# Bias and map of the fourth row group by GpSimd, in a binarised 3x3 convolution on one core

## The chip, the cores and the metric

The program runs on one core of a Trainium2 chip. The metric is the device time of one execution in microseconds (us). Three executions of the kernel before took 914.83, 915.45 and 915.15 us, a median of 915.15 us.

## The reference

The input `x` has 16 images of 256 channels and 56 x 56 pixels, in f32. It is normalised over groups of 8 channels, then by batch statistics over all images. The sign `t` (+1 or -1) of the result goes through a 3x3 convolution with 256 output channels, a bias is added, and every pixel is multiplied by a map that has one value per pixel for all channels. The input is added at the end:

```
t  = sign(xn)
xc = clip(xn, -1, 1)
y  = conv3x3(t, conv_w) + conv_b
beta_map = (box3x3(sum_c(xc * t)) + beta) / (box3x3(sum_c |t|) + beta)
out = x + y * beta_map
```

The change concerns the last two steps of `y`: "add the bias, multiply by the map".

## The kernel before, in words

**Start.** Up to 134 us the images are loaded once for their statistics, and the weights are scaled and transformed. GpSimd does 30 operations on the weights there, all done by about 101 us.

**Images and groups.** Each image has four groups g = 0..3: g % 2 is the half of the channels (256 = 2 x 128 partitions), g // 2 the upper or lower 28 rows. A group is a 128 x 1568 f32 tile `y[:, g]`. The convolution is done in a transformed form over the rows: TensorE makes six planes per group in three pairs, 24 matmuls each. In the steady loop PE takes, for each g of image n, `first(n, g)`, `third(n, g - 1)` and `second(n, g)`: 72 matmuls a slot, 288 an image. After `first(n, 0)` (in image 1 after `third(0, 3)`) it makes `quarter_sums` (L688), two small matmuls for the map of image n. `first(n, g)` waits until the accumulator pair that it writes into has been read: `y03_done` at 4n + g - 1, which is the end of `ends(n, g - 2)` on VectorE (L735, 736).

**VectorE (DVE)** works off a written list. Its pieces are:
- `transform(n + 1, g)` (L994 to 1016): the six input planes of a group of the next image, from the tile `T`; f16 operations, most with two inputs in SBUF.
- `mid(n, g)` (L1055 to 1069): two of every four output rows of a group, from ScalarE's snapshots `sn` of the accumulators. It waits for `y_out[g]`, the previous image's store out of `y[:, g]`.
- `ends(n, g)` (L1071 to 1079): the other two rows, read from the accumulators in PSUM and the tile `ds` in SBUF. It signals `y03_done`.
- `finish(n, g)` (L1081 to 1088): bias and map in one operation over 128 x 1568, in place in `y[:, g]`. It signals `scaled`.
- `pair_sum` (L1030) and `fold` (L1037): sums for the map; `beta_map(n)` (L1043 to 1052): the map of image n. It waits for `crow`, which comes by two DMAs from the quarter sums.

The order in the steady loop (`begin` and `proceed`) for an image n is: finish(n-1, 1), transform(n, 3), mid(n-1, 3), ends(n-1, 3), beta_map(n); finish(n-1, 2), transform(n+1, 0), mid(n, 0), ends(n, 0), pair_sum(n+1, 0); **finish(n-1, 3)**, fold(n+1, 0), transform(n+1, 1), mid(n, 1), ends(n, 1); finish(n, 0), pair_sum(n+1, 1), transform(n+1, 2), mid(n, 2), ends(n, 2), fold(n+1, 1). In image 1, `beta_map(1)` comes after ends(1, 0).

**ScalarE (ACT)** makes the signs, the tile `T`, the absolute values, and the snapshots.

**GpSimd (POOL)** only issues DMAs after the start. Its queue runs over s = 4n + g: wait until `y[:, g]` is scaled, issue the DMA that adds `x` to it (L385), then wait until the add before that has landed and issue its store to `out` (L380).

**SyncE (SP)** issues the loads of `x`, the DMAs of the sums, and the loads of the map into `bmap`: `map_load(n, 1)`, the lower half, waits until finish(n-1, 3) is done with the half that it overwrites (L289 to 295).

The last image's group 3 has code of its own (`last_mid`, `last_end`, `last_finish`).

Of the kernel before, what the change touches and what calls it, by code (L numbers as in the profile page):

```python
# [49 lines left out]
def conv_preact(nc, x, w_t, consts, sum_rows, map_rows, out):  # L50
# [6 lines left out]
    with ExitStack() as ctx:  # L57
# [3 lines left out]
        def sem(name):  # L61
            return ctx.enter_context(nc.semaphore(name))
# [96 lines left out]
            sem(s) for s in ("first_done", "second_done", "third_done", "snap1", "snap2"))  # L159
        ds_done, mid_done, y03_done, scaled, last_added = (  # L160
            sem(s) for s in ("ds_done", "mid_done", "y03_done", "scaled", "last_added"))

        WA = 13
        WP = 15
# [5 lines left out]
        def at_least(eng, s, value):  # L170

            if not (isinstance(value, int) and value <= 0):
                eng.wait_ge(s, value)
# [62 lines left out]
        @block.sync  # L236
        def _(sp):
            def stat_load(k):

                m, a, c = stat_image(k)  # L240
                if k >= BUFFERS:
                    block_read(sp, k - BUFFERS)
                sp.dma_start(stat_buffer(k), x_rows[m, c]).then_inc(s_in[k % BUFFERS], 16)

            def load_rows(src, g):

                h = g // 2
                first = (HR - 1) * W * h
                sp.dma_start(xb[:, g % 2, h], src[g % 2, :, first:first + XR * W]).then_inc(x_in[g], 16)

            stat_load(0)
            stat_load(1)
            for c in range(CT):
                sp.dma_start(wt[:, c], w_v[:, c].rearrange("p (a b o) -> p a b o", a=3, b=3)).then_inc(w_in[c], 16)
            for k in range(2, 2 * NI - 2):
                stat_load(k)
            for c in range(CT):
                block_read(sp, (2 * NI - 3) // BUFFERS * BUFFERS + c)
                for g in (c, 2 + c):
                    first, at = (HR - 1) * W * (g // 2), (UPPER - 1 + g // 2) * W  # L260
                    for lo, hi, s in ((0, at, x_upper[g]), (at, XR * W, x_in[g])):
                        sp.dma_start(xb[:, c, g // 2, lo:hi], x_rows[0, c][:, first + lo:first + hi]).then_inc(s, 16)

            def crow_load(m):

                sp.wait_ge(cs8_ready, m + 1)
                sp.dma_start(sum_rows[m, W:W + H * W].rearrange("(k f) -> k f", f=SQ), cs98[:, :])\
                  .then_inc(cs_stored, 16)
                sp.wait_ge(cs_stored, 16 * m + 16)
                at_least(sp, vsum_ready, m)  # L270
                sp.dma_start(crow[:, :, 1:W + 1], row_windows[m].rearrange("r (k w) -> r k w", w=W))\
                  .then_inc(crow_in, 16)

            def load(n, src, g):

                sp.wait_ge(u_ready, 4 * n + g + 4)
                sp.wait_ge(abs_done, 4 * n + g + 5)
                load_rows(src, g)

            def first_load(g):  # L280

                if g:
                    sp.wait_ge(u_ready, g)
                else:
                    sp.wait_ge(u0_ready, 1)
                sp.wait_ge(abs_done, g + 1)
                load_rows(x_rows[1], g)

            def map_load(n, h):  # L289

                if h:
                    at_least(sp, scaled, 4 * n)
                sp.dma_start(bmap[:, h, :],
                             map_rows[n:n + 1, h * HPX:(h + 1) * HPX].to_broadcast([P, HPX]))\
                  .then_inc(bmap_in[h], 16)

            def map_store(n):

                sp.wait_ge(bm_ready, n + 1)
                sp.dma_start(map_rows[n].rearrange("(r w) -> r w", w=W), bm[:, :]).then_inc(bm_stored, 16)  # L300
                sp.wait_ge(bm_stored, 16 * n + 16)

            def image(n, ahead=None):

                crow_load(n)
                if ahead is not None:
                    load(n, ahead, 0)
                map_store(n)
                map_load(n, 0)
                if ahead is not None:  # L310
                    load(n, ahead, 1)
                map_load(n, 1)
                if ahead is not None:
                    load(n, ahead, 2)
                if ahead is not None:
                    load(n, ahead, 3)

            for g in range(G4):
                first_load(g)
            sp.wait_ge(zeros_in, 16)  # L320
            image(0, x_rows[2])
            for n in range(1, NI - 2):
                image(n, x_rows[n + 2])
            image(NI - 2)
            image(NI - 1)

            sp.wait_ge(last_added, 1)
            sp.dma_start(out_v[NI - 1, 0, 1], y[:, 2]).then_inc(last_out[2], 16)
            for k, (lo, hi) in enumerate(LAST_ROWS):
                sp.wait_ge(last_added, k + 2)  # L330
                sp.dma_start(quads(out_v[NI - 1, 1, 1])[:, :, lo:hi].rearrange("p q i w -> p q (i w)"),
                             quads(y[:, 3])[:, :, lo:hi].rearrange("p q i w -> p q (i w)")).then_inc(last_out[k], 16)
            for g in range(G4):

                sp.wait_ge(y_out[g], 16 * (NI - (g > 1)))
            for k in range(3):
                sp.wait_ge(last_out[k], 16)


        @block.gpsimd  # L340
        def _(pool):
            done = [0]

            def after_own():

                pool.wait_ge(w_pool, done[0])

            def signal(ins):
                ins.then_inc(w_pool, 1)
                done[0] += 1  # L350


            pool.wait_ge(wscale, 1)
            for ci in range(CT):
                w0, w1, w2 = (wt[:, ci, d] for d in range(3))
                E, PP, QQ, G0, G2, HH = (wtmp[:, k] for k in range(6))
                for dy in range(3):
                    signal(nc.gpsimd.tensor_tensor(
                        wt[:, ci, dy], wt[:, ci, dy], scl[:, None, :].to_broadcast([P, 3, C]), ALU.mult))
                if ci:  # L360
                    pool.wait_ge(w_act, WA * ci)
                after_own()
                signal(nc.gpsimd.tensor_tensor(E, w0, w2, ALU.add))
                after_own()
                signal(nc.gpsimd.tensor_tensor(PP, E, w1, ALU.add))
                signal(nc.gpsimd.tensor_tensor(QQ, E, w1, ALU.subtract))
                pool.wait_ge(w_act, WA * ci + 3)
                signal(nc.gpsimd.tensor_tensor(G0, G0, G2, ALU.add))
                after_own()
                signal(nc.gpsimd.tensor_tensor(G2, G0, HH, ALU.add))  # L370
                signal(nc.gpsimd.tensor_tensor(HH, HH, G0, ALU.subtract))

                for o, (k, src) in enumerate(((0, w0), (5, w2), (1, PP), (2, QQ), (3, G2), (4, HH))):
                    pool.wait_ge(w_act, WA * ci + 7 + o + 1)
                    signal(nc.gpsimd.tensor_tensor(U[:, ci, 1, k], src, U[:, ci, 0, k], ALU.subtract))
            def store(s):

                n, g = divmod(s, G4)
                pool.wait_ge(x_added[g], 16 * n + 16)
                pool.dma_start(out_v[n, g % 2, g // 2], y[:, g]).then_inc(y_out[g], 16)  # L380

            for s in range(G4 * NI - 2):
                n, g = divmod(s, G4)
                pool.wait_ge(scaled, s + 1)
                pool.dma_start(y[:, g], x_v[n, g % 2, g // 2], accum_op=ALU.add).then_inc(x_added[g], 16)  # L385
                if s:
                    store(s - 1)
            store(G4 * NI - 3)


# [408 lines left out]
        def _(dve):  # L799
# [289 lines left out]

            def add_x(g):  # L1090

                dve.wait_ge(scaled, G4 * NI - 3 + g)
                nc.vector.tensor_tensor(y[:, g], y[:, g], own_rows(g), ALU.add).then_inc(last_added, 1)

            def last_mid():
# [32 lines left out]
            def last_finish(k):  # L1128
# [3 lines left out]
                dve.wait_ge(bmap_in[1], 16 * NI)  # L1132
                nc.vector.scalar_tensor_tensor(out=part(y[:, 3]), in0=part(y[:, 3]), scalar=vec[:, 2, 1:2],  # L1133
                                               in1=part(bmap[:, 1]), op0=ALU.add, op1=ALU.mult).then_inc(scaled, 1)
                dve.wait_ge(scaled, G4 * NI + k)
                nc.vector.tensor_tensor(part(y[:, 3]), part(y[:, 3]), part(own_rows(3)), ALU.add)\  # L1136
                  .then_inc(last_added, 1)

# [33 lines left out]
            def proceed(n, a, map_after=False):  # L1172
                before = lambda g, back: (n, g - back) if g >= back else (n - 1, 4 + g - back)
                for g in range(1, G4):
                    finish(*before(g, 3))
                    if g == 3:
                        pair_sum(n + 1, 1)
                    if g == 2:
# [28 lines left out]
            finish(last - 1, 2)  # L1207
            mid(last, 0)
            ends(last, 0)
            finish(last - 1, 3)  # L1210
            mid(last, 1)
            ends(last, 1)
            finish(last, 0)
# [46 lines left out]
```

## Time and profile before

| | |
|---|---|
| median of three executions | 915.15 us |
| the profiled execution's own time | 915.17 us |
| its span (first to last instruction) | 913.4 us |
| PE busy | 783.5 us, 86% |
| DVE busy | 767.3 us, 84% |
| ACT busy | 647.2 us, 71% |
| POOL busy | 139.7 us, 15% |
| mean granted clock | 0.939 |

The span is the time from the first to the last instruction of the profiled execution; 1.8 us of its own time lie around it. A busy share is an average over the start, the loop and the tail, which have different limits; POOL's counts the issuing of its DMAs.

### The profile page before, as it was taken

How to read it: one execution, taken by the hardware profiler on the slowest of the kernel's cores; microseconds unless marked ns; L12 is line 12 of the kernel's file. 1: busy time of each engine (PE TensorE's matmuls, PEld its weight loads, DVE VectorE, ACT ScalarE, POOL GpSimd, SP SyncE). 2: the span in 40 equal slices, each digit the busy share in tenths (PEclk: the TensorE clock that was granted, in tenths of full speed). 3: DMA queues.
4: the chain of work that ended last, by engine and by line, in shares of the span. 5: the costliest groups of instructions: out<-in, count | busy, mean ns of one | idle time of the engine just before them, and what ended most of it. 6: DMA issues, size and time to landing. Idle time of an engine off the chain costs nothing.

```text
span 913.4 us, 12806 instructions
## 1 busy us (share of the span) xinstructions
PE 783.5 (86%) x4722; PEld 468.0 (51%) x4722; DVE 767.3 (84%) x1193; ACT 647.2 (71%) x516; POOL 139.7 (15%) x158
## 2 busy tenths in 40 slices
PE   2100019999999999999999999999999999999996
PEld 2100015555555555555555555555555555555554
DVE  4899689999797888888888889797979797979756
ACT  2365638889696978777777777788878696969411
POOL 0089400011011111111111001111111110101011
PEclk9655559999999999999999999999999999999999
DMA  9999962399897888878888879796959696867578
GB/s 381 429 429 427 427 271 78 122 262 269 253 277 218 242 258 241 227 254 229 250 236 228 266 195 305 171 327 157 319 153 307 183 298 195 287 177 213 142 215 246
DMA packets 44874, 232.06 MB, mean 254 GB/s; under 512 B 10928, under 2 KB 11952, under 8 KB 40752
## 3 DMA queue, kind: packets, MB, share of 16 engines
q0 software_dynamic: 17856, 99.56, 41.9%
q1 hardware_dynamic: 26800, 132.05, 38.8%
q8 instruction: 14, 0.23, 0.1%
q10 hardware_dynamic: 192, 0.12, 0.0%
q14 instruction: 12, 0.10, 0.0%
HBM read 179.92 MB, written 51.79 MB: 254 GB/s over the span
## 4 chain that ended last, share of the span: by engine, by line
PE 72%; DVE 1%; DMA 1%; issue 1%; ACT 1%; DVEq 0%; ACTq 0%
PE acc L702 72%; DMA sum_rows<-cs 1%; DVE y L1133 0%; DMA crow<-sum_rows 0%; ACT r L519 0%; DVE y L1076 0%; ACT low L494 0%; PE low L688 0%; ACT r L525 0%; DVE y L1123 0%; DVE D L1008 0%; DVE ds L1060 0%; DVE y L1136 0%; ACT sn L637 0%; DVE ds L1104 0%
## 5 line engine op out<-in xcount | busy, mean ns | idle before, releaser
L702 PE MATMUL acc<-V,U 128*128 128x385 f16 (+1 forms) x4608 | 761.7, 328 | 0.9 <-DVE y L1076 0.4
L702 PEld LDWEIGHTS acc<-V,U 128*128 128x128 f16 x4608 | 449.9, 98 | 308.5 <-issue 1.5
L545 ACT ACTIVATE sn<-acc,inv_s 128x784 f32<-128x784 f32 x126 | 114.4, 908 | 162.7 <-PE acc L702 158.5
L385 POOL DMA_DIRECT2D y<-x x62 | 53.3, 859 | 702.5 <-DVE y L1087 689.1
L504 ACT ACTIVATE T<-low 128x2352 f16<-128x2352 f32 x60 | 127.3, 2122 | 0.9 <-DVE D L1008 0.9
L1087 DVE SCALAR_TENSOR_TENSOR y<-y,cst,bmap 128x1568 f32<-128x1568 f32 x63 | 115.5, 1833 | 0.1
L519 ACT ACTIVATE r<-xb,ab 128x1568 f32<-128x1568 f32 x64 | 106.6, 1690 | 5.5 <-ACT low L494 4.0
L494 ACT ACTIVATE low<-xb,ab 128x1624 f32<-128x1624 f32 x60 | 102.2, 1703 | 0.2
L508 ACT ACTIVATE T<-T 128x1568 f16<-128x1568 f16 x58 | 87.6, 1510 | 1.9
L662 PE MATMUL low<-mv,cst 128*128 128x32 f32 x2 | 0.6, 396 | 85.0 <-DVE mv L822 85.0
L1008 DVE TENSOR_TENSOR D<-T 128x1568 f16<-128x1568 f16 x60 | 58.3, 972 | 13.9 <-ACT T L508 13.8
L1060 DVE SCALAR_TENSOR_TENSOR ds<-sn 128x784 f32<-128x784 f32 x63 | 60.9, 967 | 4.0 <-ACT sn L545 4.0
L1037 DVE TRANSPOSE_TENSOR_REDUCE quarter<-ssum 128x49 f32<-128x1568 f32 x32 | 57.7, 1803 | 0.1
L1030 DVE SCALAR_TENSOR_TENSOR ssum<-r 128x1568 f32<-128x1568 f32 x32 | 57.1, 1785 | 0.3
L380 POOL DMA_DIRECT2D out<-y x62 | 50.0, 807 | 12.3 <-DMA y<-x 10.8
L525 ACT ACTIVATE r<-r 128x1568 f32<-128x1568 f32 x32 | 48.4, 1511 | 1.0
L1000 DVE TENSOR_SCALAR T<-T 128x784 f16<-128x784 f16 x60 | 21.3, 355 | 30.0 <-ACT T L504 30.0
L1065 DVE SCALAR_TENSOR_TENSOR y<-sn,ds 128x392 f32<-128x392 f32 x63 | 35.8, 568 | 10.9 <-DMA out<-y 4.5
L662 PEld LDWEIGHTS low<-mv,cst 128*128 128x128 f32 x2 | 0.5, 309 | 85.1 <-issue 85.1
L1076 DVE SCALAR_TENSOR_TENSOR y<-acc,inv_s,ds 128x392 f32<-128x392 f32 x63 | 39.0, 618 | 3.9 <-PE acc L702 3.9
L1043 DVE TENSOR_REDUCE vsum<-crow 56x58 f32<-56x174 f32 x16 | 5.5, 346 | 40.3 <-DMA crow<-sum_rows 40.3
L834 DVE BATCH_NORM_STATS2 st<-xb 128x6 f32<-128x448 f32 x63 | 34.1, 605 | 6.2 <-DMA xb<-x 6.1
(153 smaller groups left out, 517.8 us busy)
## 6 DMA issues: line engine op xcount, KB each, us to landing
xb<-x SPq DMA_DIRECT2D x60, 812.0 KB, 6.6
y<-x POOLq DMA_DIRECT2D x62, 784.0 KB, 8.5
out<-y POOLq DMA_DIRECT2D x62, 784.0 KB, 9.6
bmap<-map_rows SPq DMA_DIRECT2D x32, 784.0 KB, 6.5
xb<-x SPq DMA_DIRECT2D x10, 1568.0 KB, 18.7
y<-x SPq DMA_DIRECT2D x10, 1568.0 KB, 18.0
r<-x SPq DMA_DIRECT2D x5, 1568.0 KB, 18.0
sn<-x SPq DMA_DIRECT2D x5, 1568.0 KB, 19.0
```

The source lines that it names most:

```text
L385: pool.dma_start(y[:, g], x_v[n, g % 2, g // 2], accum_op=ALU.add).then_inc(x_added[g], 16)
L494: nc.scalar.activation(signs[:, 1:1 + XR], by_row(xb[:, c, g // 2]), ACT.Sign, scale=ab[:, a, 0, c:c + 1], bias=ab[:, a, 1, c:c + 1])\
L504: nc.scalar.activation(taps[:, 2:8].rearrange("p k (w q) -> p k w q", q=Q), row_taps(g), ACT.Relu, scale=2.0).then_inc(t_ready, 1)
L508: nc.scalar.activation(taps8, taps[:, 2:6], ACT.Copy, scale=4.0, bias=-3.0).then_inc(t8_ready, 1)
L519: nc.scalar.activation(r[:, c, 0:HPX], own_rows(g), ACT.Abs, scale=ab[:, a, 0, c:c + 1], bias=ab[:, a, 1, c:c + 1]).then_inc(abs_done, 1)
L545: nc.scalar.activation(kept, sums, ACT.Copy, scale=inv_s[:, b:b + 1]).then_inc((snap1, snap2)[half], 1)
L702: return nc.tensor.matmul(into, U[:, ci, digits, k, dx, co * P:(co + 1) * P], plane, start=(planes is FIRST and i == 0), stop=(planes is T ...
L1008: nc.vector.tensor_tensor(diff[:, 0], taps[:, 4:8], taps8, ALU.subtract).then_inc(cq_done, 1)
L1030: nc.vector.scalar_tensor_tensor(out=ssum[:, :], in0=r[:, 0, 0:HPX], scalar=1.0, in1=r[:, 1, 0:HPX], op0=ALU.min, op1=ALU.subtract).then_i ...
L1037: nc.vector.tensor_reduce(quarter[:, h, :], ssum[:, :].rearrange("p (b i) -> p b i", i=SQ), AX.X, ALU.add, apply_transpose=True).then_inc( ...
L1060: nc.vector.scalar_tensor_tensor(out=ds[:, :, :], in0=sn[:, b, 0], scalar=2.0, in1=sn[:, b, 1], op0=ALU.mult, op1=ALU.subtract).then_inc(d ...
L1087: nc.vector.scalar_tensor_tensor(out=y[:, g], in0=y[:, g], scalar=vec[:, 2, b:b + 1], in1=bmap[:, h], op0=ALU.add, op1=ALU.mult).then_inc( ...
```

## The change

The bias and map of group 3 of images 0 to 14 become two operations of GpSimd (`finish_3`): a tensor_scalar that adds the bias in place, a wait for its own signal, and a tensor_tensor that multiplies by the map in place. VectorE's finish(n, 3) goes. GpSimd starts with them when it comes to s = 4n + 3 in its queue and group 3's rows are complete; it no longer waits for VectorE there. `scaled` counts three groups an image, and the new `scaled_3` the fourth; the waits of SyncE and of the tail are adapted. Group 3 of the last image stays with VectorE.

```diff
             def map_load(n, h):
                 if h:
-                    at_least(sp, scaled, 4 * n)
+                    at_least(sp, scaled, 3 * n)
+                    at_least(sp, scaled_3, n)
...
+            def finish_3(n):
+
+                pool.wait_ge(mid_done, 4 * n + 4)
+                pool.wait_ge(y03_done, 4 * n + 4)
+                nc.gpsimd.tensor_scalar(y[:, 3], y[:, 3], vec[:, 2, 1:2], None, ALU.add).then_inc(raised, 1)
+                pool.wait_ge(raised, n + 1)
+                pool.wait_ge(bmap_in[1], 16 * n + 16)
+                nc.gpsimd.tensor_tensor(y[:, 3], y[:, 3], bmap[:, 1], ALU.mult).then_inc(scaled_3, 1)
+                pool.wait_ge(scaled_3, n + 1)
...
             for s in range(G4 * NI - 2):
                 n, g = divmod(s, G4)
-                pool.wait_ge(scaled, s + 1)
+                if g == 3:
+                    finish_3(n)
+                else:
+                    pool.wait_ge(scaled, 3 * n + g + 1)
                 pool.dma_start(y[:, g], x_v[n, g % 2, g // 2], accum_op=ALU.add).then_inc(x_added[g], 16)
...
             def add_x(g):
-                dve.wait_ge(scaled, G4 * NI - 3 + g)
+                dve.wait_ge(scaled, (G4 - 1) * NI - 2 + g)
...
-                dve.wait_ge(scaled, G4 * NI + k)
+                dve.wait_ge(scaled, (G4 - 1) * NI + 1 + k)
...
                 for g in range(1, G4):
-                    finish(*before(g, 3))
+                    if g != 2:
+                        finish(*before(g, 3))
...
             ends(last, 0)
-            finish(last - 1, 3)
             mid(last, 1)
```

## Rows read from the trace of the kernel before

**Rows 1.** The page's first part: busy time, share of the span, instructions.
```profile
span 913.4 us, 12806 instructions
PE 783.5 (86%) x4722; PEld 468.0 (51%) x4722; DVE 767.3 (84%) x1193; ACT 647.2 (71%) x516; POOL 139.7 (15%) x158
```
**Rows 2.** Windows of one image's length: busy us (instructions) of each engine, granted clock.
```profile
431.00:478.50 47.50, 47.50 (x292) 28.33 (x291) 40.56 (x57) 37.42 (x29) 5.67 (x8) 1.00 0.83 240
```
**Rows 3.** The chain that ended last, in order of time: start us, us, what.
```profile
307.14 1.17 DVE y L1076 x2
308.31 0.14 issue
308.45 27.81 PE acc L702 x168
...
573.96 47.40 PE acc L702 x288
```
**Rows 4.** Matmul timeline, image 9: start us, us, what.
```profile
573.68 0.28 PE L688 MATMUL low<-cst,quarter 128*98 128x32 f32 x2
573.79 47.56 PE L702 MATMUL acc<-V,U 128*128 128x392 f16 x288
621.20 0.28 PE L688 MATMUL low<-cst,quarter 128*98 128x32 f32 x2
```
**Rows 5.** VectorE's timeline, image 9.
```profile
582.84 0.35 DVE L1043 TENSOR_REDUCE vsum<-crow 56x58 f32<-56x174 f32 x1 [2.59 <-DMA crow<-sum_rows]
583.90 1.84 DVE L1087 SCALAR_TENSOR_TENSOR y<-y,cst,bmap 128x1568 f32<-128x1568 f32 x1
...
587.59 0.57 DVE L1013 TENSOR_TENSOR V<-D 128x784 f16<-128x784 f16 x1
...
591.07 0.62 DVE L1076 SCALAR_TENSOR_TENSOR y<-acc,inv_s,ds 128x392 f32<-128x392 f32 x1
591.60 0.62 DVE L1076 SCALAR_TENSOR_TENSOR y<-acc,inv,ds 128x392 f32<-128x392 f32 x1
592.13 1.79 DVE L1030 SCALAR_TENSOR_TENSOR ssum<-r 128x1568 f32<-128x1568 f32 x1
593.84 1.85 DVE L1087 SCALAR_TENSOR_TENSOR y<-y,cst,bmap 128x1568 f32<-128x1568 f32 x1
...
597.33 0.32 DVE L1000 TENSOR_SCALAR T<-T 128x784 f16<-128x784 f16 x1
...
603.34 0.61 DVE L1076 SCALAR_TENSOR_TENSOR y<-acc,inv,ds 128x392 f32<-128x392 f32 x1
```
**Rows 6.** Matmul timeline, quarter sums of images 1, 3 and 4.
```profile
196.52 0.36 PE L688 MATMUL low<-cst,quarter 128*98 128x32 f32 x2
...
288.27 0.28 PE L688 MATMUL low<-cst,quarter 128*98 128x32 f32 x2
...
336.10 0.28 PE L688 MATMUL low<-cst,quarter 128*98 128x32 f32 x2
```
**Rows 7.** VectorE's timeline, images 1 and 3.
```profile
211.59 0.61 DVE L1076 SCALAR_TENSOR_TENSOR y<-acc,inv,ds 128x392 f32<-128x392 f32 x1
...
298.92 0.35 DVE L1043 TENSOR_REDUCE vsum<-crow 56x58 f32<-56x174 f32 x1 [3.84 <-DMA crow<-sum_rows]
```
**Rows 8.** Waits of PE, 140 to 240 us: us in total, times, longest.
```profile
PE acc L702 <- DVE y L1076: 0.4, 1, 0.4
```
**Rows 9.** GpSimd's groups by form: busy us, mean ns | idle before.
```profile
L385 POOL DMA_DIRECT2D y<-x x62 | 53.3, 859 | 702.5 <-DVE y L1087 689.1 <-issue 13.4
L371 POOL TENSOR_TENSOR V<-V 128x768 f32<-128x768 f32 x2 | 3.6, 1806 | 0.0
```
**Rows 10.** VectorE's groups by form.
```profile
L1087 DVE SCALAR_TENSOR_TENSOR y<-y,cst,bmap 128x1568 f32<-128x1568 f32 x63 | 115.5, 1833 | 0.1
L1022 DVE TENSOR_SCALAR u<-xb,AB,neg_b 128x1624 f16<-128x1624 f32 x1 | 1.1, 1124 | 0.0
```
**Rows 11.** GpSimd's timeline, image 9.
```profile
586.03 0.86 POOL L385 DMA_DIRECT2D y<-x  x1 [12.60 <-DVE y L1087]
586.59 0.87 POOL L380 DMA_DIRECT2D out<-y  x1
595.98 0.85 POOL L385 DMA_DIRECT2D y<-x  x1 [8.53 <-DVE y L1087]
596.90 0.56 POOL L380 DMA_DIRECT2D out<-y  x1
```
**Rows 12.** VectorE's groups, 44 to 62 us, beside GpSimd's operations.
```profile
L834 DVE BATCH_NORM_STATS2 st<-sn 128x6 f32<-128x448 f32 x7 | 3.8, 601 | 0.0
```
**Rows 13.** VectorE's groups, 104 to 120 us, GpSimd idle.
```profile
L834 DVE BATCH_NORM_STATS2 st<-y 128x6 f32<-128x448 f32 x14 | 7.5, 604 | 3.2 <-DMA y<-x 3.2
```
**Rows 14.** Windows in the tail and in the warm-up; the third number from the end is the granted clock.
```profile
909.00:913.40 4.40, 0.00 (x0) 0.00 (x0) 1.19 (x2) 0.00 (x0) 0.00 (x0) 0.81 0.63 182
```

More of the change, by code:

```diff
@@ L161, in conv_preact @@
             sem(s) for s in ("ds_done", "mid_done", "y03_done", "scaled", "last_added"))
+        raised, scaled_3 = sem("raised"), sem("scaled_3")
         WA = 13
```

## The prediction

> **What bounds the kernel now.** I read the engines' busy times first: PE 86%, DVE 84% [rows 1]. These average over the start, so next came windows of one image's length in the loop: PE is busy for all of 47.50 us at full clock, DVE for 40.56, ACT for 37.42, POOL for 5.67 [rows 2]. The chain of waits says the same: unbroken pieces of 288 matmuls, 47.40 us each [rows 3]. TensorE sets the time from 225 us on. A faster VectorE gives it nothing; a later one costs, once it is later than its margin.
>
> So the question is how large that margin is. In image 9 the quarter sums start at 573.68 us and the next ones 47.52 us later; the 288 matmuls between take 47.41 us, 0.1646 us each [rows 4]. `first(9, 2)` stands 120 matmuls after the quarter sums, at 573.79 + 19.75 = 593.54 us. It needs `ends(9, 0)`, whose second operation ends at 591.60 + 0.61 = 592.21 us [rows 5]. Image 3 shows what happens without margin: the last operation of ends(3, 0) ends at 308.31, PE starts 0.14 us later at 308.45 [rows 3], and that image takes 336.10 - 288.27 = 47.83 us [rows 6] where image 9 takes 47.52. So the result must be there 0.14 us early, and the margin in image 9 is 593.54 - 0.14 - 592.21 = **1.2 us**. The stretch before it is tied to PE: the map's `crow` lands at 582.84 us, 9.16 us behind the quarter sums, and from there VectorE has no gap up to 592.21, 9.4 us [rows 5]. A delay in that stretch is not worked off before PE needs the result, and as `crow` follows PE's quarter sums, the stretch begins as late as PE does in the next image: each image pays anew. In image 3 `crow` came 10.65 us behind [rows 6, 7], hence no margin. In image 1, where the sums stand 24 matmuls later, ends(1, 0) ends at 212.20 [rows 7] and is needed at 196.52 + 0.11 + 96 x 0.1646 - 0.14 = 212.29 [rows 6]: 0.1 us.
>
> **The change, part by part.**
>
> *Taken from VectorE:* 15 operations of 1833 ns [rows 10], 27 us. In image 9 it is the one at 593.84 us [rows 5], behind ends(9, 0), so it widens the margin of the next slot alone. PE waits there once, for 0.4 us in image 1 [rows 8]: worth 0.4 us; elsewhere the matmuls hide it.
>
> *Added to GpSimd, the product:* a tensor_tensor over 768 f32 takes 1806 ns [rows 9], so 1568 take 1.806 x 1568 / 768 = 3.7 us.
>
> *Added to GpSimd, the bias:* no row shows a tensor_scalar there. From above, 3.7 us, the rate of the tensor_tensor; from below 1.1 us, VectorE's one-input f32 operation over 1624 [rows 10]. The nearest row is GpSimd's own, and the new operation has one input stream where that has two: I take half of it, 1.85 us. The Trainium skill (GPSIMD Engine Reference, 4.1 Engine selection) says that GpSimd's one-input elementwise work runs at roughly line rate, and its section 3 gives 1.03 cycles an element at 1.2 GHz, by which I estimate 1.35 us; the forecast would then be about 7 us lower.
>
> *Where they run:* GpSimd's queue comes to group 3 of image 8 after the add of group 2 (586.03 us) and the store behind it, which ends at 587.46 [rows 11]. Group 3's rows are then long complete. So the two operations begin at 587.5 us, amid VectorE's gapless stretch (L1013 starts at 587.59), and need 1.85 + 3.7 = 5.55 us: to 593.1, past the end of ends(9, 0).
>
> *What stands queued behind:* the add of x (595.98 us before) and the store of group 2 (596.90) [rows 11]. Alone, GpSimd would be done by 593.3, so both go out no later than before; cost nothing. SyncE's map load for the lower half waits for the same point, also no later. Should GpSimd take 5 us more, both go out some 2 us late, with the whole slot of 11.9 us until `mid` of the next group needs the store.
>
> *What they do to VectorE:* this is the disputed term. Between 587.5 and 591.07 us nearly all its operations (V<-D, ds, the two of `mid`) read two tiles in SBUF. The trace has no such operation beside GpSimd's arithmetic. It has only one-input ones: bn_stats takes 601 ns beside GpSimd's tensor_tensors and 604 ns with GpSimd idle [rows 12, 13], no loss. For two inputs the loss L lies between nothing and the whole 5.55 us (VectorE standing still while GpSimd works); a gain is excluded, as the removed operation lies behind ends(n, 0). Only the first 1.2 us are free, so four fifths of the interval cost time. I take the upper end, L = 5.55 us: GpSimd and VectorE each work in place over whole rows, and what one has in one-input operations is no measure of it. The Trainium skill (SBUF — State Buffer, Who interferes with whom) says that a VectorE instruction with two SBUF inputs contends with a GpSimd instruction that reads SBUF, since its second input comes through a read interface that they share, and that whichever starts second waits for the whole of the first. The one-input rows agree with that page's other half, that a one-input instruction outside the two-port modes is not held up; no row here shows the two-input case.
>
> *The sum:* images 2 and 4 to 14 (12 images): 12 x (5.55 - 1.2) = 52.2 us. Image 1: 5.55 - 0.1 = 5.45. Image 3: 5.55. Image 15 has no transforms, and its ends wait for PE: 0. The wait in image 1: -0.4. Together 62.8 us. Against the profiled execution, 915.17 us (span 913.4 and 1.8 around it; 0.02 over the median), that is **978 us**. With the bias at 1.1 us it is 14 x 0.75 = 10.5 less, 967.5; with 3.7 us 25.9 more, 1004.
>
> **The rivals.** 0.2% of the time, 1.8 us, is about what a measurement of this kernel can tell from no change.
>
> *A. Hidden, not slower.* GpSimd and VectorE do not hold each other up, or VectorE keeps precedence while its operations follow without a gap. Then GpSimd's bias falls in the free place, the two operations of `ends` at 591.07 [rows 5], which read one tile from PSUM. It ends at 592.9, holds pair_sum (592.13) by 0.8 us; the product begins behind pair_sum at 594.7 and ends at 598.4, beside the fold; the next transform begins 1.1 us later than its 597.33, and ends(9, 1), 603.95 before, ends at 605.0 where PE needs it at 593.54 + 11.85 - 0.14 = 605.25. PE never waits. The time is 915.2 less at most 0.4 + 0.3 us: 914.5 to 915.3. It decides if L in the first slot stays under 1.2 us. For it: the bn_stats rows and that VectorE leaves no gap where GpSimd begins.
>
> *B. Partly.* The two share, or only the bias gets in before ends(n, 0): L about 1.85 us gives 12 x 0.65 + 1.75 + 1.85 - 0.4 = 11 us, 926 us; L = 3.7 us (only the product, or a loss of two thirds) gives 12 x 2.5 + 3.6 + 3.7 - 0.4 = 36.9, 952 us. Range 917 to 955.
>
> *C. The clock falls too.* The granted clock was 1.00 through the loop; in the last 4.4 us, in which PE has no matmul left, it averages 0.81 [rows 14], so it fell from 2.4 to 1.2 GHz in there. Whether a pause of 4.4 us between matmuls does so no row shows. A stretch at 1.2 GHz loses half its length: 4 us of it behind every pause would cost 14 x 2 = 28 us more, 1006 us.
>
> *D. Faster.* Nothing on PE's chain is taken away beyond 0.7 us, under 0.2%.
>
> **How the numbers follow.** Full hold-up 0.40 (its own range 965 to 1003), B 0.20, C 0.07, A 0.31, D 0.02. The interval argument (four fifths of L cost time) speaks for slower, the one-input rows for A. Slower is then 0.67, same 0.31, faster 0.02. The predicted time is that of the likeliest case, 978 us. The range takes in A, B and the bounds of the bias's length: 914.5 to 1000 us; it is wide because the two main cases lie 60 us apart. If PE is held up, 1% or 7% hangs on how much of the 5.55 us is lost.
>
> **What would show it.** Windows over one image of the changed kernel: PE no longer full, some 4.4 us idle an image, released by L1076 at the start of `first(n, 2)`; quarter sums 51.9 us apart instead of 47.5. On VectorE the operations L1013 to L1067 of that slot stretched, or gaps of 1.9 and 3.7 us between them; the same operations in the other three slots unchanged. GpSimd's two new rows about 1.85 and 3.7 us. The forecast is wrong if two-input operations beside GpSimd keep their 0.57 and 0.97 us, or if GpSimd's rows are stretched in place of VectorE's, with the period still at 47.52 us.

## The result, and the profile after

The changed kernel takes **1016.9 us** (median of four executions, 1014.85 to 1017.6) against 915.09 us: a ratio of 1.1109, 95% interval 1.1095 to 1.1122. It is slower, by 102 us where 63 us were forecast, and outside the range. The profiled execution has a span of 1015.8 us against 913.4.

The page's first part:

```profile
span 1015.8 us, 12851 instructions
PE 811.7 (80%) x4722; PEld 475.3 (47%) x4722; DVE 838.4 (83%) x1178; ACT 648.9 (64%) x516; POOL 260.4 (26%) x188
```

VectorE has 15 instructions fewer than in [rows 1] and is busy 71 us longer. TensorE, with the same 4722, is busy 28 us longer. Both must be explained. A window from one quarter sums to the next, which answers to [rows 2] (in the same columns):

```profile
578.40:633.10 54.70, 49.44 (x292) 28.83 (x291) 45.16 (x56) 37.55 (x29) 13.74 (x10) 0.94 0.75 209
```

An image takes 54.7 us instead of 47.5, PE stands still for 5.3 of them, and the granted clock averages 0.94 instead of 1.00. The matmul timeline of the same image, against [rows 4]:

```profile
578.43 0.28 PE L703 MATMUL low<-cst,quarter 128*98 128x32 f32 x2
578.54 19.91 PE L717 MATMUL acc<-V,U 128*128 128x392 f16 x120
603.73 29.59 PE L717 MATMUL acc<-V,U 128*128 128x392 f16 x168 [5.26 <-DVE y L1091]
633.15 0.28 PE L703 MATMUL low<-cst,quarter 128*98 128x32 f32 x2
```

The pause lies where it was looked for: 120 matmuls behind the quarter sums, at `first(n, 2)`, ended by `ends(n, 0)` (now L1091). The 168 matmuls behind it take 29.59 us, where a piece of that length at full clock takes 27.81. VectorE's timeline there, against [rows 5]:

```profile
591.52 0.97 DVE L1023 TENSOR_TENSOR D<-T 128x1568 f16<-128x1568 f16 x1
592.58 3.64 DVE L1028 TENSOR_TENSOR V<-D 128x784 f16<-128x784 f16 x1
596.14 0.55 DVE L1029 TENSOR_TENSOR V<-D 128x784 f16<-128x784 f16 x1
596.62 0.55 DVE L1030 TENSOR_TENSOR V<-D 128x784 f16<-128x784 f16 x1
597.10 4.26 DVE L1075 SCALAR_TENSOR_TENSOR ds<-sn 128x784 f32<-128x784 f32 x1
601.47 0.57 DVE L1080 SCALAR_TENSOR_TENSOR y<-sn,ds 128x392 f32<-128x392 f32 x1
```

and GpSimd's, against [rows 11]:

```profile
592.17 4.55 POOL L382 TENSOR_SCALAR y<-y,cst 128x1568 f32<-128x1568 f32 x1
596.80 3.72 POOL L385 TENSOR_TENSOR y<-y,bmap 128x1568 f32<-128x1568 f32 x1
600.82 0.89 POOL L400 DMA_DIRECT2D y<-x  x1 [0.30 <-POOL y L385]
```

Two VectorE operations are stretched, one beside each GpSimd operation: L1028 from 0.57 to 3.64 us and L1075 from 0.97 to 4.26 us. The hold-up is 3.07 + 3.29 = **6.36 us**; less the margin of 1.2 us that leaves 5.2 us, and the pause is 5.26. The others keep their lengths: each GpSimd operation holds one VectorE operation. The two GpSimd operations take 8.27 us, and the holds are 1.91 us less: VectorE's next two-input operation comes 0.41 and 0.30 us after they begin, and it is let go before they end, L1028 some 1.07 us before (596.22 - 0.57 = 595.65 against 596.72) and L1075 some 0.13 us before.

The clock in that pause and behind it (windows; the third number from the end is the granted clock):

```profile
598.00:600.00 2.00, 0.46 (x3) 0.07 (x1) 2.00 (x1) 1.50 (x2) 2.00 (x1) 1.00 1.04 264
600.00:602.00 2.00, 0.00 (x0) 0.00 (x0) 1.89 (x3) 1.97 (x2) 1.70 (x3) 0.64 1.00 403
602.00:603.70 1.70, 0.00 (x0) 0.01 (x1) 1.70 (x5) 0.97 (x1) 0.29 (x1) 0.50 0.99 413
603.70:605.00 1.30, 1.27 (x5) 0.61 (x6) 1.30 (x1) 0.00 (x0) 0.00 (x0) 0.50 0.97 386
608.00:609.00 1.00, 1.00 (x8) 0.60 (x7) 0.91 (x2) 0.00 (x0) 0.00 (x0) 1.00 1.10 226
```

PE stops at 598.5 us, the clock is at half (1.2 GHz) before it starts again at 603.7, and is back at 2.4 GHz by 608.

**The account.** PE's waits for L1091 add up to 74.3 us (15 times). The 14 pieces of 168 matmuls behind the long pauses take 29.30 to 30.60 us, 26.7 us more in all than 14 x 27.81. Together they make 101.0 us of the 102.4 by which the span is longer.

### The profile page after: what moved, and what is told of

Same layout as the page of the kernel before. It is cut to its first block and busy times, and to the rows that moved or that the text cites. A ratio compares the mean times of both kernels' runs of the same rounds, so it can differ in the third digit from the quotient of the medians.

```text
span 1015.8 us, 12851 instructions
## 1 busy us (share of the span) xinstructions
PE 811.7 (80%) x4722; PEld 475.3 (47%) x4722; DVE 838.4 (83%) x1178; ACT 648.9 (64%) x516; POOL 260.4 (26%) x188
## 5 line engine op out<-in xcount | busy, mean ns | idle before, releaser
L717 PE MATMUL acc<-V,U 128*128 128x385 f16 (+1 forms) x4608 | 790.5, 335 | 74.9 <-DVE y L1091 74.3
L717 PEld LDWEIGHTS acc<-V,U 128*128 128x128 f16 x4608 | 457.6, 100 | 403.5 <-issue 109.3
L1075 DVE SCALAR_TENSOR_TENSOR ds<-sn 128x784 f32<-128x784 f32 x63 | 108.7, 1725 | 2.8 <-ACT sn L560 2.8
L1102 DVE SCALAR_TENSOR_TENSOR y<-y,cst,bmap 128x1568 f32<-128x1568 f32 x48 | 88.0, 1833 | 0.1
L1028 DVE TENSOR_TENSOR V<-D 128x784 f16<-128x784 f16 x60 | 77.1, 1285 | 5.6 <-DVE D L1023 0.5
L382 POOL TENSOR_SCALAR y<-y,cst 128x1568 f32<-128x1568 f32 x15 | 68.3, 4555 | 0.0
L1045 DVE SCALAR_TENSOR_TENSOR ssum<-r 128x1568 f32<-128x1568 f32 x32 | 57.2, 1787 | 9.7 <-ACT r L540 8.0
L1052 DVE TRANSPOSE_TENSOR_REDUCE quarter<-ssum 128x49 f32<-128x1568 f32 x32 | 57.9, 1808 | 0.6
L385 POOL TENSOR_TENSOR y<-y,bmap 128x1568 f32<-128x1568 f32 x15 | 55.6, 3706 | 1.3
L1091 DVE SCALAR_TENSOR_TENSOR y<-acc,inv_s,ds 128x392 f32<-128x392 f32 x63 | 39.2, 622 | 19.7 <-PE acc L717 19.7
L1015 DVE TENSOR_SCALAR T<-T 128x784 f16<-128x784 f16 x60 | 21.3, 355 | 39.6 <-ACT T L519 39.6
L1080 DVE SCALAR_TENSOR_TENSOR y<-sn,ds 128x392 f32<-128x392 f32 x63 | 39.7, 630 | 7.6 <-DMA out<-y 1.3
```

What stands on the lines that cost most here:

```text
L382: nc.gpsimd.tensor_scalar(y[:, 3], y[:, 3], vec[:, 2, 1:2], None, ALU.add).then_inc(raised, 1)
L717: return nc.tensor.matmul(into, U[:, ci, digits, k, dx, co * P:(co + 1) * P], plane, start=(planes is FIRST and i == 0), stop=(planes is T ...
L1028: nc.vector.tensor_tensor(V[:, a, c, 2:5:2, h], diff[:, :, 2], diff[:, :, 1], ALU.add)
L1052: nc.vector.tensor_reduce(quarter[:, h, :], ssum[:, :].rearrange("p (b i) -> p b i", i=SQ), AX.X, ALU.add, apply_transpose=True).then_inc( ...
L1075: nc.vector.scalar_tensor_tensor(out=ds[:, :, :], in0=sn[:, b, 0], scalar=2.0, in1=sn[:, b, 1], op0=ALU.mult, op1=ALU.subtract).then_inc(d ...
L1102: nc.vector.scalar_tensor_tensor(out=y[:, g], in0=y[:, g], scalar=vec[:, 2, b:b + 1], in1=bmap[:, h], op0=ALU.add, op1=ALU.mult).then_inc( ...
```

## The experiments

Ratios are against the kernel before, on the same chip. **Theory H**: VectorE's operations with two inputs in SBUF stand still while GpSimd reads SBUF; PE pauses by the hold-up less the margin; in a long enough pause the clock falls as well.

### One operation alone

*bias_only* puts only the bias on GpSimd:

```diff
+                if g == 3:
+                    pool.wait_ge(mid_done, 4 * n + 4)
+                    pool.wait_ge(y03_done, 4 * n + 4)
+                    nc.gpsimd.tensor_scalar(y[:, 3], y[:, 3], vec[:, 2, 1:2], None, ALU.add).then_inc(raised, 1)
                 pool.wait_ge(scaled, s + 1)
...
+                if g == 3:
+                    dve.wait_ge(raised, n + 1)
+                    nc.vector.tensor_tensor(y[:, g], y[:, g], bmap[:, h], ALU.mult).then_inc(scaled, 1)
+                    return
```

> Only the bias of group 3 on GpSimd; VectorE keeps the product as one two-input operation at its old place. Theory H (VectorE's two-input operations stand still while GpSimd reads SBUF; PE's pause is the hold-up less the margin of 1.2 us): L1013's counterpart held by 3.1 us as in the changed kernel, pause 1.9 us in 12 images, about 3.0 in images 1 and 3, 28 us in all: 944 us, clock stays up. If the clock falls in pauses of 1.9 us too, up to 970. Rival Q (the loss comes from GpSimd's queue: adds and stores go out late behind the two operations): GpSimd is done before VectorE's product, queue times as before, so 915 us. Rival O (no hold-up by GpSimd's first operation, only by the product): 915 us.

*product_only* is the changed kernel without its tensor_scalar.

> Only the product on GpSimd, the bias of group 3 left out. Theory H: the 3.7 us tensor_tensor starts where the bias started; one VectorE operation held by about 3.0 to 3.3 us, pause 1.8 to 2.1 us, 12 x 1.95 + 3.1 x 2 = 30 us: 945 us, clock up. The two single runs then make 59 us together, and the 102 us of the changed kernel hold some 43 us more: 17 us from the margin being used once instead of twice (14 x 1.2), and 26 to 28 us of clock. Rival Q: 915 us.

Measured: bias_only 949.97 us, ratio 1.0375 (1.0345 to 1.0405); product_only 956.33 us, 1.0431 (1.0398 to 1.0463). The one stretched operation of each, and GpSimd's beside it, first in bias_only:

```profile
607.68 4.57 POOL L388 TENSOR_SCALAR y<-y,cst 128x1568 f32<-128x1568 f32 x1
...
608.11 3.65 DVE L1018 TENSOR_TENSOR V<-D 128x784 f16<-128x784 f16 x1
```

then in product_only:

```profile
610.12 3.84 POOL L383 TENSOR_TENSOR y<-y,bmap 128x1568 f32<-128x1568 f32 x1
...
610.57 3.84 DVE L1026 TENSOR_TENSOR V<-D 128x784 f16<-128x784 f16 x1
```

The holds, 3.08 and 3.27 us, are those of the changed kernel. PE's waits for `ends` add up to 27.5 and 30.1 us, as theory H says (28 and 30). Q and O, which expected 915 us of a run with one operation, fall. Both runs are some us over the forecast because of the clock: in three and in six of the pauses. The matmul timeline of product_only has both kinds, with nearly the same pause:

```profile
517.63 27.81 PE L715 MATMUL acc<-V,U 128*128 128x392 f16 x168 [2.04 <-DVE y L1089]
...
567.45 29.49 PE L715 MATMUL acc<-V,U 128*128 128x392 f16 x168 [2.14 <-DVE y L1089]
...
668.57 27.81 PE L715 MATMUL acc<-V,U 128*128 128x392 f16 x168 [2.29 <-DVE y L1089]
```

The granted clock is 1.00 in the 3.4 us behind the pause of 2.04 us and averages 0.55 in the 3.55 us behind that of 2.14. A fall costs 1.68 us there. Of the pauses of 1.5 to 1.9 us in these two runs none brought one, of those of 2.0 to 2.3 us some did, of those of 2.7 us and more all.

### Reads or writes

*write_only* has memsets of `y[:, 3]` in place of the two operations, so bias and map of group 3 are left out and its values overwritten:

```diff
-                nc.gpsimd.tensor_scalar(y[:, 3], y[:, 3], vec[:, 2, 1:2], None, ALU.add).then_inc(raised, 1)
+                for k in range(3):
+                    nc.gpsimd.memset(y[:, 3], 0.5).then_inc(raised, 1)
...
-                nc.gpsimd.tensor_tensor(y[:, 3], y[:, 3], bmap[:, 1], ALU.mult).then_inc(scaled_3, 1)
+                nc.gpsimd.memset(y[:, 3], 0.5).then_inc(raised, 1)
...
+                nc.gpsimd.memset(y[:, 3], 0.5).then_inc(scaled_3, 1)
```

> GpSimd's two operations replaced by five memsets of the same tile, one waiting for the other: it writes 128x1568 five times and reads nothing (bias and map of group 3 are left out, its values overwritten). Theory H (the shared part is the read side): VectorE's operations beside it keep 0.57 and 0.97 us, no pause, 915 us. Rival W (any GpSimd access to SBUF holds two-input VectorE operations): hold-ups of several us, pauses, over 940 us.

914.58 us, ratio 0.9995 (0.9985 to 1.0004). GpSimd writes for some 7.5 us an image at the same place, and VectorE beside it keeps its lengths:

```profile
586.56 4.66 POOL L383 MEMSET y<- 128x1568 f32 x3
...
587.02 0.57 DVE L1031 TENSOR_TENSOR V<-D 128x784 f16<-128x784 f16 x1
...
588.46 0.97 DVE L1078 SCALAR_TENSOR_TENSOR ds<-sn 128x784 f32<-128x784 f32 x1
```

So it is not GpSimd's queue, its semaphores, the work taken from VectorE or its writes, and GpSimd's reading is what is left. A GpSimd operation that only reads was not run. Rival W falls.

### The clock by itself

*filled_pause* is the changed kernel with small matmuls in the pause. They write into columns of a bank of the other accumulator pair that nobody reads. The kernel's results come out altered all the same, and why was not looked into; the number and order of its other operations stay:

```diff
                 for g in range(G4):
+                    if g == 2:
+                        pe.wait_ge(snap2, 4 * n + 2)
+                        for _ in range(52):
+                            nc.tensor.matmul(acc[:, 1, 0, N:N + 120], U[:, 0, 0, 0, 0, 0:P],
...
```

> The changed kernel with 52 small matmuls (120 columns, into a part of an accumulator bank that nobody uses) before first(n, 2), behind the wait for the snapshot, to keep PE at work for most of the pause. If the 2.0 us by which the 168 matmuls behind each pause are longer is the clock: granted clock 1.00 through the loop, 168 matmuls in 27.7 us, 14 x 2.0 = 28 us less, and about 4 us more in image 15, where there is no pause to fill: 993 us. If the slow matmuls come from something else (their operands' reads disturbed by GpSimd or VectorE catching up): 1017 to 1021 us with the clock at 1.00.

994.63 us, ratio 1.0869 (1.0850 to 1.0887):

```profile
534.49 2.90 PE L772 MATMUL acc<-U 128*128 128x120 f16 x52 [1.01 <-ACT sn L560]
538.68 27.81 PE L717 MATMUL acc<-V,U 128*128 128x392 f16 x168 [1.29 <-DVE y L1097]
```

and the window of that image, from one quarter sums to the next:

```profile
513.50:566.40 52.90, 50.60 (x345) 31.03 (x344) 45.00 (x56) 37.42 (x29) 13.76 (x10) 1.00 0.76 216
```

VectorE is as late as before, but PE has two short pauses in place of a long one, the granted clock stays at 1.00, and the 168 matmuls are back at 27.81 us in 13 of the 14 images (in image 2 they take 29.49). 22 us are gone: 26.7 us of the longer pieces, less 1.7 us for image 2 and 3.9 us of wait and fillers in image 15, which has no pause; the pauses with their fillers are some 1 us shorter in all. The second part of the loss is the clock.

### The same two operations at another place

*earlier* has `finish_3(n)` ahead of the add of group 2:

```diff
-                if g == 3:
+                if g == 2:
                     finish_3(n)
-                else:
+                if g < 3:
                     pool.wait_ge(scaled, 3 * n + g + 1)
```

> The same two operations on GpSimd, but ahead of the add of group 2 in its queue: the bias then starts behind ends(n-1, 3), where VectorE waits 2.9 us for crow. Theory H: that pause and the one-input reduction take most of the bias's hold; about 0.4 us is left on the 56-row operations of the map, and the product holds one more operation (finish of group 2, or what follows) by 2.9 to 3.1 us. Hold-up 3.3 to 3.5, pause 2.1 to 2.3 us an image, as in product_only; 12 x 2.2 + 7 = 33 us and the clock in half of the pauses, 10 to 15 us: 945 to 965 us. Rival Q (what costs is how late GpSimd's queue gets to adds and stores): here add and store of groups 1 and 2 go out up to 4 us later than in the changed kernel, so slower than its 1017 us.

*later* holds them back until `ends(n, 0)` is done:

```diff
-                pool.wait_ge(y03_done, 4 * n + 4)
+                pool.wait_ge(y03_done, 4 * n + 5)
```

> The same two operations, held back until ends(n, 0) is done. Theory H: the hold-up comes behind ends(n, 0), so the first margin is not touched, and the next one is 1.4 + 1.8 us (the operation taken from VectorE lies there) = 3.2 us. The bias starts with pair_sum, which is already under way, and the fold has one input: no hold. The product holds one operation of the transform by 2.5 to 2.9 us. Under 3.2: hardly a pause, 915 to 920 us. If GpSimd's bias itself has to wait for pair_sum, the holds are 1.7 us more: pause 1.3 us, 933 us. Rival N (what counts is GpSimd's busy time beside VectorE's, wherever it lies): 1000 us or more.

*split* has the bias at the first of these places and the product at the second.

> The same two operations, apart: the bias behind ends(n-1, 3), ahead of the add of group 2, where VectorE waits for crow; the product behind ends(n, 0). Theory H: holds of 0.4 us before ends(n, 0), margin 1.2; then the product starts beside pair_sum and the one-input fold, hold 0 to 1.5 us, margin 3.2. No pause but for some us in images 1 to 3, where VectorE has no gap: 915 to 919 us, with all 15 operations taken from VectorE and both put on GpSimd as in the changed kernel. Rival N: 1000 us or more.

| | us | ratio (95%) | PE's waits for `ends`, us |
|---|---|---|---|
| earlier | 972.17 | 1.0629 (1.0611 to 1.0647) | 32.9 |
| later | 970.99 | 1.0611 (1.0594 to 1.0629) | 31.6 |
| split | 920.38 | 1.0054 (1.0038 to 1.0071) | 3.4 |

Nothing was done here but to move GpSimd's work, and the loss goes from 102 us to 57 and 56, and to 5 us. Rival N (GpSimd's busy time counts wherever it lies) falls, and Q again. In *earlier*, pause and hold are as expected (2.1 to 2.2 us in most images, 4.4 and 2.6 in images 1 and 3; the map's first small operation is held by 0.25 us on average, one of the transform by 3.19). But the clock fell in 12 of the 14 pauses, not in half, and 972 us lie above the 945 to 965 expected. In *later*, too, it fell in 12 of the 14. *split* lies 1.4 us above its 915 to 919; its two pauses for `ends`, 1.25 and 2.10 us, are in image 1.

*later* is the larger miss: 915 to 920 or 933 us were expected. Its VectorE timeline between ends(n, 0) and the next held operation, and GpSimd's:

```profile
570.61 0.62 DVE L1091 SCALAR_TENSOR_TENSOR y<-acc,inv,ds 128x392 f32<-128x392 f32 x1
571.25 1.79 DVE L1045 SCALAR_TENSOR_TENSOR ssum<-r 128x1568 f32<-128x1568 f32 x1
573.08 1.81 DVE L1052 TRANSPOSE_TENSOR_REDUCE quarter<-ssum 128x49 f32<-128x1568 f32 x1
575.84 1.54 DVE L1015 TENSOR_SCALAR T<-T 128x784 f16<-128x784 f16 x1 [0.95 <-ACT T L519]
577.41 3.76 DVE L1020 TENSOR_TENSOR D<-T 128x784 f16<-128x784 f16 x1
...
571.40 5.75 POOL L382 TENSOR_SCALAR y<-y,cst 128x1568 f32<-128x1568 f32 x1 [6.02 <-DVE y L1091]
577.24 3.51 POOL L385 TENSOR_TENSOR y<-y,bmap 128x1568 f32<-128x1568 f32 x1
```

Three things were missing in my sum. The hold works **in both directions**: pair_sum (L1045) was first, and GpSimd's bias takes 5.75 us where it takes 4.24 beside a VectorE that waits for crow (GpSimd's groups by form in *earlier*, below). That pushes it into the transform, where L1015, a tensor_scalar with **one** input, is held too (1.54 us for 0.35). And part of the time that the removed operation gave back is no margin, as VectorE now waits 0.95 us for `T`. 0.95 + 1.19 + 3.19 = 5.3 us against the 3.2 us of margin leave 2.1, the pause measured. The one-input fold (L1052) is not held.

```profile
L382 POOL TENSOR_SCALAR y<-y,cst 128x1568 f32<-128x1568 f32 x15 | 63.6, 4239 | 96.9 <-DVE y L1091 96.9
```

The Trainium skill (SBUF — State Buffer, Who interferes with whom) says that whichever starts first has the shared access for the whole instruction, that a tensor_scalar in a two-port mode contends as well, and that a tensor_reduce never does. The rows agree with the first for the bias behind pair_sum and, to within 0.15 us, for L1015 and L1020 behind GpSimd. They do not agree with it for a two-input operation beside the bias, which was let go 1.07 us before the bias ended in the changed kernel, and likewise in *bias_only*; there the measurement decides. L1015's hold of 1.19 us fits the second if it ran in such a mode, which no trace names. The fold's row, a TRANSPOSE_TENSOR_REDUCE, fits the third. *write_only* agrees with the same section's statement that a GpSimd operation that only writes does not contend with a two-input one.

*split_from_1* leaves image 0's group 3 with VectorE, so that image 1 has nothing of GpSimd in it (counts of the semaphores adapted):

```diff
-                if g == 2:
+                if g == 2 and n:
...
-                    if g != 2:
+                    if g != 2 or map_after:
                         finish(*before(g, 3))
```

> As split, but image 0's group 3 stays with VectorE at its old place, so that image 1, where VectorE has no gap, has nothing of GpSimd in it. Theory H: the 5.3 us by which split was slower lie in image 1 alone; with them gone 914.5 to 915.5 us, no difference to the kernel before that can be measured, with 14 of 15 operations moved. If split's loss came from something steady (queue, DMA issue, the map's load): nearly 920 us again.

914.87 us, ratio 1.0001 (0.9991 to 1.0010), with the matmuls unbroken again:

```profile
573.61 47.56 PE L720 MATMUL acc<-V,U 128*128 128x392 f16 x288
```

Bias and map of group 3 are on GpSimd in 14 of the 15 images, and nothing is lost. Nothing is gained either: PE was full before.

### The scalar, and the size of a piece

*bias_imm* has the immediate 0.5 as the bias of group 3 in place of the column.

> The changed kernel with 0.5 as an immediate in place of the bias column read from SBUF (so group 3 gets another bias). If GpSimd's tensor_scalar took 4.55 us because of the scalar that it reads from a tile: nearer to 1.9 to 3.7 us, and the first hold-up shorter by as much. If it is the operation itself: 4.5 us again, and 1017 us.

1014.6 us (one execution); the tensor_scalar takes 4.49 us where the column's takes 4.55. The price is the operation's.

*pieces* has each of the two operations in four pieces of 392 columns, *halves* in two of 784. The bias in *pieces*:

```diff
...
+                for k in range(4):
+                    q = slice(k * N, (k + 1) * N)
+                    nc.gpsimd.tensor_scalar(y[:, 3, q], y[:, 3, q], vec[:, 2, 1:2], None, ALU.add).then_inc(raised, 1)
...
```

> The changed kernel with each of GpSimd's two operations in four pieces of 392 columns. If a whole-instruction hold is what costs, VectorE gets in one operation between two pieces, and its holds are short and many: eight holds of 0.7 to 0.9 us, the sum 6 to 7 us again as long as VectorE's two-input operations follow each other: pause about 5 us, 1010 to 1030 us. If GpSimd's pieces are held by VectorE's in turn (as its bias was by pair_sum in the run later), part of the pieces slips behind ends(n, 0), where the margin is larger, and the time falls to 950 to 1000 us.

> As pieces, with two pieces of 784 columns in each of GpSimd's two operations. Whole operations of 1568 columns held VectorE by 3.1 us each, pieces of 392 by 0.2 to 0.3 us each. If the hold is the piece's length less about 1.1 us (the end of it, in which it writes only): a piece of 784 takes 2.0 to 2.5 us and holds 0.9 to 1.3 us; three to four of them lie before ends(n, 0), 3 to 4.5 us in all, pause 2 to 3 us with some falls of the clock: 945 to 975 us. If what counts is whether VectorE gets in between at all: 0.3 us each again, 919 us.

Measured 919.29 us, ratio 1.0048 (1.0033 to 1.0064), and 920.25 us, 1.0052 (1.0036 to 1.0069). Of *pieces* both branches of the expectation were far too high. Of *halves* the first was; the second, 919 us, came near the time, but by holds of 0.5 to 0.7 us a piece and not 0.3. In *pieces*, GpSimd's two operations and VectorE's beside them:

```profile
589.88 5.96 POOL L384 TENSOR_SCALAR y<-y,cst 128x392 f32<-128x392 f32 x4
595.92 5.48 POOL L389 TENSOR_TENSOR y<-y,bmap 128x392 f32<-128x392 f32 x4
...
590.32 0.89 DVE L1032 TENSOR_TENSOR V<-D 128x784 f16<-128x784 f16 x1
...
592.09 1.27 DVE L1079 SCALAR_TENSOR_TENSOR ds<-sn 128x784 f32<-128x784 f32 x1
593.46 0.77 DVE L1084 SCALAR_TENSOR_TENSOR y<-sn,ds 128x392 f32<-128x392 f32 x1
```

Now the waiting is GpSimd's: 11.4 us for what took 8.3, while VectorE is held by 0.32 + 0.30 + 0.20 = 0.8 us before ends(n, 0), under the margin. In *halves* it is 0.68 + 0.51 = 1.2 us, just the margin, and fragile: in image 5 of the profiled execution (926.95 us, and one other like it among six) GpSimd got in first four times before ends(5, 0), the holds add up to 5.8 us, and PE paused:

```profile
410.91 30.14 PE L721 MATMUL acc<-V,U 128*128 128x392 f16 x168 [4.33 <-DVE y L1095]
```

What is left in *pieces*, 4.6 us of the span, has two parts. PE waits 3.0 us for `ends` in images 1 to 3, where there is little or no margin. And the program ends 8.7 us behind its last matmul instead of 6.9: in the last image VectorE waits 3.56 us (at 899.03 us) for the store out of `y[:, 2]`, a wait that the kernel before does not have. That store stood in GpSimd's queue behind the eight pieces and went out at 887.47 us; before, it went out at 881.15, in an image that began 2.85 us earlier. So the queue, rival Q, has a small part here after all. Why VectorE gets in ahead at almost every border between pieces was not isolated.

## Why the prediction was wrong, point by point

- **What bounds the kernel, and the margin of 1.2 us: right.** Pauses followed the hold-up less the margin in five runs (the changed kernel, *bias_only*, *product_only*, *earlier*, *bias_imm*), at `first(n, 2)` and anew in each image. They were larger by about a us in images 1 and 3, in *earlier* by 2.2 and 0.4.
- **Where the work lands, and what is queued behind it: right.** GpSimd's operations start in the gapless stretch. Adds and stores cost nothing in the changed kernel; only in the last image of *pieces* and *halves* did a late store cost 1.5 to 1.8 us.
- **The disputed term, full hold-up: right in kind, its size by luck** (0.40 in the forecast). VectorE did stand still, but for 6.36 us of the 8.27 that GpSimd works, not for all of it. A (hidden) and B (partly) did not happen at this place. A's second condition, VectorE keeping precedence, is what *pieces* shows, for small pieces only.
- **The price of the bias, wrong.** "The new operation has one input stream where that has two: I take half of it, 1.85 us" measured 4.55 us, 4.24 with VectorE waiting; it lies over my upper bound of 3.7 us, the rate of the two-input operation. The rule that I set beside it, one-input work at roughly line rate (the Trainium skill, GPSIMD Engine Reference, 4.1 Engine selection), is contradicted by this measurement as well. The product's price, 3.7 us, was right. The bias was 2.7 us longer than assumed and the holds were 1.9 us shorter than the two operations, and these two errors took each other out in part: the hold-up came out at 6.36 us, not 5.55, 14 x 0.8 = 11 us. With the bias alone put right and VectorE standing still for all 8.27 us, the sum would have been 14 x 2.7 = 38 us higher, which is 1016 us without any clock: the right number for a wrong reason.
- **The clock, wrong: it was a rival at 0.07 and belonged into the sum.** "Whether a pause of 4.4 us between matmuls does so no row shows" was true, but the one row that bears on it, [rows 14], shows the clock falling within 4.4 us without matmuls, and the sum put it at nothing all the same. It cost 26.7 us, the greater part of the miss; C had priced it at 28 us. 978 + 11 + 27 = 1016 us, and 1016.9 were measured.
- **The range, wrong:** it ended at 1000 us although my own bound for the bias gave 1004 and C 1006. Both errors lay on the same side and added.

## What to carry to other kernels

Before work moves to GpSimd, look at which VectorE operations lie beside it and how long until somebody needs their result, not at how busy either engine is. Here the same two operations cost 102 us in one place of the loop and 5 us in others, and nothing once image 1 was left out. Where work could not be placed beside other operations or waits, small pieces held VectorE much less than one long operation did, though pieces of 784 columns did so less reliably. And where a forecast has TensorE pause for some 5 us in each pass, the lower clock behind the pause belongs into the sum: here it came behind all 14.

## What was not expected of the hardware

- GpSimd's tensor_scalar over 128x1568 f32 takes 4.24 us by itself, longer than its tensor_tensor (3.51 us in *later*), with the scalar from SBUF or immediate (4.55 and 4.49 us at the same place). A memset of the same tile takes 1.40 us (*write_only*).
- A two-input VectorE operation held by the bias goes on 1.07 us before the bias ends (in *bias_only* 1.06), and L1029 ran beside the bias's last 0.6 us. Held by the product it goes on only 0.13 us before the end. The one-input L1015 in *later* was let go 0.12 us before the end of the same bias. Why they differ was not isolated.
- GpSimd is held as VectorE is: 5.75 us instead of 4.24 for a bias that found pair_sum at work.
- The clock was at half within a pause of 5 us, and of pauses of 2.0 to 2.3 us in one kernel some lowered it and some did not.
